# A transformer layer on one Trainium2 core: sixteen transposes in one block, and the scores ahead of the projection of v

## The reference, cut to what matters

```
x    = ln(src) * (1 + scale) + shift            # scale, shift from the timestep
q, k, v = x @ Wq + bq, x @ Wk + bk, x @ Wv + bv # 16 heads of 32
s    = q @ k.T / sqrt(32) + attention_bias      # 16 x 128 x 128, masked with -inf
p    = softmax(s)
x    = x + (p @ v) @ Wo + bo
out  = x + gelu2((ln(x) * g2 + beta2) @ W1 + b1) @ W2 + b2   # 512 -> 2048 -> 512
```

## Time and profile before

| | before |
|---|---|
| median of 3 runs | 2562.18 us |
| profiled execution | 2562.13 us |
| its span, first to last instruction | 2560.3 us |
| mean granted TensorE clock | 0.994 of full |
| TensorE busy (matmul) | 2490.9 us, 97% |
| VectorE, ScalarE, GpSimd busy | 51%, 38%, 38% |

### The profile page before, as it was taken

The page is one execution under the profiler, slowest core; times in us unless marked ns, Lnnn a source line. Parts: engine busy times, 40 slices in busy tenths (PEclk is TensorE's granted clock), DMA queues, the critical chain, the costliest instruction groups (busy, mean ns, idle before and its releaser), DMA issues.

```text
span 2560.3 us, 46325 instructions
## 1 busy us (share of the span) xinstructions
PE 2490.9 (97%) x16402; PEld 2080.1 (81%) x16402; DVE 1308.1 (51%) x2515; ACT 965.0 (38%) x3183; POOL 970.8 (38%) x830
## 2 busy tenths in 40 slices
PE   4999999999999999799999999999999999999999
PEld 3888888888888888578888888888888888888887
DVE  4777777777777776554233333323323333332332
ACT  2666666666666666632111121121111112112111
POOL 3777777777777777521011011101101101110100
PEclk8999999999999999999999999999999999999999
DMA  7444444444444443231000000000000000000000
GB/s 228 126 134 134 135 134 137 135 135 134 136 134 136 136 139 106 75 123 50 6 28 33 33 0 33 33 0 33 33 9 24 33 33 0 33 33 0 33 17 17
DMA packets 205879, 187.33 MB, mean 73 GB/s; under 512 B 20224, under 2 KB 159616, under 8 KB 205696
## 3 DMA queue, kind: packets, MB, share of 16 engines
q1 hardware_dynamic: 205696, 184.99, 23.1%
HBM read 151.14 MB, written 33.82 MB: 72 GB/s over the span
## 4 chain that ended last, share of the span: by engine, by line
PE 56%; DMA 0%; DVE 0%; POOL 0%; issue 0%; SPq 0%; ACT 0%; DVEq 0%
PE psY L1025 9%; PE psY L1027 9%; PE psY L1026 9%; PE psH L1027 9%; PE psH L1026 9%; PE psH L1025 9%; PE turn L207 1%; DMA b_bc<-in_b 0%; POOL r L940 0%; DVE r L1000 0%; DVE wo_hi L985 0%; DVE w_lo L990 0%; POOL r L180 0%; DVE w_lo L993 0%; DVE wo_hi L983 0%
## 5 line engine op out<-in xcount | busy, mean ns | idle before, releaser
L958 ACT ACTIVATE gf<-psH,b_c 128x512 f32<-128x512 f32 x256 | 176.4, 689 | 1182.0 <-PE psH L1027 1182.0
L983 DVE CAST wo_hi<-gf 128x512 fp32r<-128x512 f32 x256 | 116.2, 454 | 878.3 <-ACT gf L958 878.3
L1025 PE MATMUL psH<-hT_hi,w_hi 128*128 128x512 f32 x1024 | 405.4, 396 | 10.9 <-DVE w_lo L990 10.9
L1025 PE MATMUL psY<-w_hi,wo_hi 128*128 128x512 f32 x1024 | 410.4, 401 | 1.3 <-DVE wo_hi L985 1.3
L1027 PE MATMUL psH<-hT_hi,w_lo 128*128 128x512 f32 x1024 | 406.0, 397 | 0.0
L1026 PE MATMUL psH<-hT_lo,w_hi 128*128 128x512 f32 x1024 | 405.3, 396 | 0.0
L1027 PE MATMUL psY<-w_hi,wo_hi 128*128 128x512 f32 x1024 | 405.0, 396 | 0.0
L1026 PE MATMUL psY<-w_lo,wo_hi 128*128 128x512 f32 x1024 | 404.4, 395 | 0.0
L618 ACT ACTIVATE s<-s,nmx 128x128 f32<-128x128 f32 x1024 | 396.1, 393 | 8.8 <-issue 5.7
L560 POOL TENSOR_TENSOR s<-s,rinv 128x512 f32<-128x512 f32 x256 | 266.1, 1040 | 231.3 <-DVE rinv L684 231.1
L553 POOL TENSOR_TENSOR bias<-bias,mneg 128x512 f32<-128x512 f32 x256 | 335.5, 1334 | 11.0 <-DVE mneg L689 11.0
(11 more groups left out here) (134 smaller groups left out, 4581.6 us busy)
## 6 DMA issues: line engine op xcount, KB each, us to landing
bias<-in_bias SPq DMA_DIRECT2D x128, 512.0 KB, 5.2
adab<-ada_rows SPq DMA_DIRECT2D x64, 512.0 KB, 5.3
xin<-in_x SPq DMA_DIRECT2D x32, 512.0 KB, 4.7
resid<-rout SPq DMA_DIRECT2D x64, 256.0 KB, 2.0
r<-resid SPq DMA_DIRECT2D x16, 1024.0 KB, 5.6
out<-r SPq DMA_DIRECT2D x64, 256.0 KB, 2.1
raw_o<-in_W SPq DMA_DIRECT2D x32, 256.0 KB, 3.0
w_ada<-in_W_ada SPq DMA_DIRECT2D x1, 2048.0 KB, 10.8
```

The costliest lines, as they stand in the source:

```text
L958: act.activation(gf[:, j % 2, :], psH[j % 2][:, :], ACT.Gelu_apprx_sigmoid, bias=b1_c[:, j:j + 1]).then_inc(gelu_done, 1)
L983: dve.tensor_copy(gT[0][:, j % 2, :], gf[:, j % 2, :]).then_inc(g_hi, 1)
L1025: pe.matmul(out_ap, sh, mh, start=start, stop=False)
```

## The change

The sixteen transposes of a batch's probabilities come in one block, behind chunk 1. The scores of batch t+1 come directly behind the turn of x, and the projection of v of batch t+2 follows them. ScalarE copies the four groups of transposed probabilities in a row behind its copy of chunk 1. VectorE takes all four groups of scores first, then `add_bv` (which stood near the end of the step before, and now stands behind the next step's scores), then the first maxima, the inverse sums of the last group, the residual and the mask.

```diff
@@ scalar
-                if on.prev:
-                    copy_pT(t - 1, 0)
-                    copy_pT(t - 1, 1)
                 if on.attn:
                     exps(t, b, 0)
                 if on.proj:
                     copy(*kq, 1)
                 if on.prev:
-                    copy_pT(t - 1, 2)
-                    copy_pT(t - 1, 3)
+                    for g in range(G):
+                        copy_pT(t - 1, g)
@@ vector
                 if on.attn:
-                    scores(t, p, b, 0)
-                    scores(t, p, b, 1)
+                    for g in range(G):
+                        scores(t, p, b, g)
+                if on.proj if b else on.attn:
+                    add_bv(t + 1, (u + b) % 2, 1 - b)
+                if on.attn:
+                    highest(t, b, 0)
+                if on.prev:
+                    invert(t - 1, 1 - b, G - 1)
                 if on.done:
                     add_residual(t - 2, p - 1, (u - 1) % UNROLL, b)
                 if on.mask:
                     negate_mask(p + b, 1 - b)
                 if on.attn:
-                    scores(t, p, b, 2)
-                    highest(t, b, 0)
-                if on.prev:
-                    invert(t - 1, 1 - b, G - 1)
-                if on.attn:
-                    scores(t, p, b, 3)
                     for g in range(1, G):
                         highest(t, b, g)
...
                 if on.turn:
                     norm.low(dve, p + 2, u % 2, b)
-                if on.proj:
-                    add_bv(t + 2, (u + 1) % 2, b)
@@ tensor
                     project_t(q, x, 0, wm, done)
-                if on.prev:
-                    transpose_p(t - 1, 1 - b, 0, on.attn)
-                    transpose_p(t - 1, 1 - b, 1, on.attn)
...
                     project_t(q, x, 1, wm, done)
                 if on.prev:
-                    transpose_p(t - 1, 1 - b, 2, on.attn)
-                    transpose_p(t - 1, 1 - b, 3, on.attn)
+                    for g in range(G):
+                        transpose_p(t - 1, 1 - b, g, on.attn)
...
                 if on.turn:
                     norm.transpose(pe, p + 2, (u + 2) % UNROLL, b)
+                if on.mask:
+                    qk(t + 1, u + b, 1 - b)
                 if on.proj:
                     at_least(pe, copied, q * G + 3)
                     project_v(t + 2, x, b)
-                if on.mask:
-                    qk(t + 1, u + b, 1 - b)
```

## The result

The changed kernel takes 2577.37 us (median of 5 runs, 2576.17 to 2579.13), the kernel before, run beside it, 2563.41 us (5 runs, 2561.35 to 2566.48). The ratio is 1.0054, with a 95% interval of 1.0040 to 1.0069: slower by more than 0.2%, where 2552.5 us and a gain had been forecast. The profiled execution took 2577.62 us with a span of 2575.6, so it stands for the median, and it is 15.3 us of span above the profiled one of before.

A forecast was written before the change was run, and what follows sets the result against it. TensorE's matmuls, filling 97% of the span, were taken as the bound. From 2562.13 us, -11.0 - 2.0 - 2.9 + 3.0 + 2.0 + 1.3 = -9.6 gave 2552.5 us; own range 2547 to 2557, overall 2546 to 2561.

The forecast's parts named there:

- Part 1: TensorE's steady steps: one exit from the transposes fewer saves 0.10 us a step.
- Part 2: TensorE's steady steps: scores ahead of v save 0.10 us a step, 0.08 at the least, 0.18 at the most.
- The ceiling: Highest cost taken for the new passage from the turn of x to the scores: 0.10 us, as from v to scores.
- Part 3: Twelve steps whose second eight transposes wait for GpSimd: these waits go, -2.0 us.
- Part 4: Queues in a steady step: the new order's four possible waits all have slack or are free, no cost.
- a to d: Odd-step scores: 0.3 us slack; context split: free; chunk 0 behind `add_bv`: 1.2 us; chunk 1 behind the residual: 0.3 us.
- Part 5: Five backward branches: VectorE's 2.66 us stall now delays `add_bv` and chunk 0, 0.6 us each, +3.0 us (0 to +5).
- Part 6: Start: chunk 0 waits for v, +2.0 us; TensorE's clock may fall in the idle time, +1.3 us (0 to 2.6).
- Part 7: End, steps 62 to 64: scores done earlier shorten the chains, -2.9 us (0 to -4).
- Rival 1: Steady steps: exits cost the same wherever they stand, only Part 1 saves, 0.10 us a step; 2558.0 us, chance 0.17.
- Rivals 2, 3 and 4: 2: saves 0.32 a step, 2545.9 us, chance 0.13; 3: ScalarE late with q, 2561.5 us, chance 0.08; 4: rival 4.
- rival 4: VectorE's queue: `add_bv` sets chunk 0 in every step, 0.5 us beyond the slack in 60 steps, +30, 2582 us; chance 0.12.

The follow-up runs named there:

- e1_tblock: The kernel before with only the sixteen transposes, and ScalarE's four copies of them, in one block; 2567.4 us, ratio 1.0015.
- e2_qkfirst: The kernel before with only TensorE's order of scores and v exchanged, scores directly behind the turn of x; 2586.89 us, ratio 1.0095.
- e6_turn: e4_cut with the turn of x directly behind the transposes, so that context and scores products adjoin; 2562.7 us, ratio 1.0000 to the kernel before.
- e3_dveold: The changed kernel with VectorE's order of the kernel before; 2599.44 us, ratio 1.0146 to the kernel before.
- e4_cut: The changed kernel with only VectorE's loop branch moved half a step, ahead of an odd step's context cast; 2557.12 us, ratio 0.9984 to the kernel before.

## Why the prediction was wrong, point by point

**Part 1, the exit: wrong.** The step that failed is "Coming out does: 0.21, so 0.094 more". The number is right, the reading is not. Transposes run 0.109 apart, so eight last 0.87, but the first matmul behind them already starts after 0.79, and the second comes 0.09 late. The exit takes 0.09 later what it gave 0.08 earlier. Both together cost 0.01, and that is what one exit fewer saves. The upper bound of 0.13 for chunk 1 had 0.04 of pace in it, and the pace changed sides: chunk 1 went from 0.118 to 0.114, chunks 2 and 3 from 0.114 to 0.118. By their lengths, chunk 1 saved 0.13, the block gave back 0.08, and chunks 2 and 3 lost 0.09: +0.04 instead of -0.10 (e1_tblock: +0.03). That the pace would move with the order, no row could tell.

**Part 2, the scores ahead of v: wrong, by the same reading.** The term that failed is the saving of 0.08 in "The first after the turn of x costs 486.27 to 486.58 = 0.31, so 0.08 more". v's first product had started 0.03 behind the last transpose of x and not 0.11, so it was 0.08 early, and its 0.31 only gave that back: this passage cost nothing. The ceiling held: the scores start 0.20 behind the last transpose (497.44 to 497.64), 0.09 more than the transposes' own pace, and "the first scores' start 0.2 behind the last turn's" came true. So 0.10 was saved where v went into the scores and 0.09 paid for the new passage. By lengths it is 0.175 more from the turn to the scores and 0.16 less for the three products: +0.02 instead of -0.10. The Trainium skill ("TensorE: Matmul & The Clock Gate", "Step-by-step: what each phase is for") has a weight load pulled ahead of running matmuls where row groups do not conflict, or where it goes to the background weight buffer. The trace agrees with the first: the load of v had started at 486.24, ahead of its matmul at 486.27, and that of the scores starts with its matmul, 0.17 us after TensorE's loads fell idle. (Before, it came at 489.19, 0.08 ahead of the end of v's last product in the profile, and not when that was through.)

```profile
497.64 0.98 PEld L774 LDWEIGHTS psS<-kf,qf 32*128 32x128 f32 x32 [0.17 <-issue]
```

The rule gives no size for it. In step 60, which has no turn of x, the change does save time: 15.18 instead of 15.34. Parts 1 and 2 together: +0.06 a step instead of -0.20, **14 us of the 24.9 between forecast and median.**

**Part 3, the waits of the transposes: right**, -2.0, but not for the whole reason. None is left. The inverse sums come earlier, as said, and in the ordinary steps the mask operation no longer meets GpSimd either (e2_qkfirst); the part did not have it.

**Part 4, the slack of the queues: right**, a to d. v ended 1.3 us ahead of chunk 0 (reckoned 1.2). The thinnest, q's copy with 0.3, held, and e6_turn, which puts 0.6 less between chunk 3 and the scores, found it: 0.33 of waiting. Part 4 took VectorE's operations at fixed lengths; e2_qkfirst and e3_dveold show that one of them grows by 1 us when GpSimd's work shifts. That it didn't here was luck.

**Part 5, the branch: right place, size too small.** VectorE's gap, start to start, was 3.32 and not 2.77, the scores came 0.7 later than reckoned, and the five steps rose by 1.4 each, not 0.6: +6.9. The bound of +5 was passed already here. What I did not price at all is what the wait does to TensorE behind it: the clock fell at three of five, about 1.6 each, +4.8. Together +11.7 instead of +3.0. e4_cut takes it away and leaves all else. I had asked for the clock at the start, where the idle time was 3.5 us, and not here, where it was 2. In both kernels VectorE stands still at all five branches; what e4_cut adds is that this costs nothing where the engine would wait anyway. The Trainium skill ("Runtime: NRT & Kernel Launch", "Instruction fetch mechanics") speaks of a forced fetch at a taken branch, and with standstills of up to 3.4 us the trace agrees.

**Part 6, the start: right mechanism, clock term too small.** The first wait was 3.46 (reckoned 3.5). The clock fell twice, behind each of the two waits, and steps 0 and 1 took 4.3 us more than in e4_cut, where it fell at neither, with the same 3.45. Without the clock the reckoning was good: from step -1 to the end of step 1 e4_cut takes 2.2 us more than the kernel before (41.91 against 39.75), for +2.0. What TensorE does ahead of that is the same, but took 0.7 us less in the changed kernel and 1.4 less in e4_cut than in the kernel before, which hides it in the table. My half of 2.6 was the mean of two outcomes, and one came, at 1.6 times the size.

**Part 7, the end: right**, -3.1 for -2.9.

**The rivals.** Rival 1 had the direction of the steps right and was too mild: it let part 1 save. Rivals 2, 3 and 4 did not happen. The time came out on the slower side, through the chain that rival 4 names, inverse sums, scores and `add_bv`, but only where the branch lengthens it, at five steps in sixty, and through the clock behind it; the rest is parts 1 and 2.

## What to carry to other kernels

A long gap between two starts is not a price by itself: look whether the gap ahead of it was short by as much, and set the whole passage against both paces before it is counted as a saving. Parts 1 and 2 both failed on this. Where work is moved on an engine, look where that engine's loop goes back, and put the branch into time in which it waits anyway; here that was worth 15 us with no instruction moved past another. A wait of 2 us on the engine that bounds the kernel can cost as much again in clock, so every new wait on it needs two prices. And where an operation's length differs between steps, look at what the other engines run at that time before it is taken as fixed.

## What the hardware showed that I had not expected

- TensorE's granted clock fell to half after waits of 2.12, 1.78 and 1.98 us at full load ahead of them, and did not after 1.88, 1.79 and, in other runs, 3.45 us. The length of the wait alone did not decide it.
- A small VectorE operation (mask to f32, 128x128, 0.22 us by itself) that starts while a GpSimd instruction runs ends only 0.08 to 0.09 us behind that instruction, in 327 cases of 327. It took up to 1.28 us, and cost about 0.45 us a step in e2_qkfirst.
- Matmuls of 256 columns in a dense row start 0.114 or 0.118 us apart at a granted clock of 1.00. In an ordinary step both paces stand side by side, and which chunk has which changes with the order; for dozens of steps with the same instructions all chunks can have the slow one. That change came at a backward branch, and in the kernel before the way back came in a step with a short wait. That these are the cause was not tried.
- Into the scores (32 rows) TensorE starts 0.20 us behind the last matmul whether that was a transpose on the whole array or a product of PV, and the first matmul of 256 or 512 columns behind a row of transposes starts 0.03 behind the last one, with the next one as much later.
- TensorE's own 0.4 to 0.8 us at each branch (`<-issue`) are there with the scores behind v and all but gone with the scores ahead of it. Why, is open.
